# Batch 0 of a fused attention and feed-forward kernel: batch 1's q and k projected ahead of the row scores, four steps of transposed scores beside the row maxima

## The reference, cut to what matters

```python
q, k, v = (embedded @ W.T + b).reshape(b, s, H, HD).transpose(0, 2, 1, 3)   # for each of Wq, Wk, Wv
...
p = jax.nn.softmax(einsum('bhqd,bhkd->bhqk', q, k) / sqrt(s), axis=-1)
p = p * jnp.triu(jnp.ones((s, s)), k=0)
z = einsum('bhqk,bhkd->bhqd', p, v)
x = layernorm(x + layernorm(x + z) * gamma + beta)
h = silu(tlin(x, w1_w, w1_s)) * tlin(x, w2_w, w2_s)
h = gelu(tlin(h, h1_w, h1_s)); h = gelu(tlin(h, h2_w, h2_s))
out = layernorm(x + tlin(h, w3_w, w3_s))
```

## Time and profile before

| what | value |
|---|---|
| median of three runs | 1188.02 us (1187.51 to 1189.85) |
| span of the profiled execution | 1187.2 us (the only time listed for it) |
| TensorE, VectorE, ScalarE, GpSimd busy | 97%, 66%, 42%, 34% |
| share of the chain that ended last | TensorE 93%, VectorE 4%, DMA 1%, ScalarE 1% |
| batch 0: first row scores | 22.5 us |
| batch 0: last row maxima end | 62.4 us |
| batch 0: first values begin, last end | 67.3, 104.7 us |
| batch 0: feed-forward begins | 117.3 us |

### The profile page before, as it was taken

The page is one execution under the profiler, slowest core; times in us unless marked ns, Lnnn a source line. Parts: engine busy times, 40 slices in busy tenths (PEclk is TensorE's granted clock), DMA queues, the critical chain, the costliest instruction groups (busy, mean ns, idle before and its releaser), DMA issues.

```text
span 1187.2 us, 18377 instructions
## 1 busy us (share of the span) xinstructions
PE 1149.0 (97%) x7311; PEld 809.2 (68%) x7311; DVE 784.1 (66%) x1276; ACT 492.9 (42%) x660; POOL 401.8 (34%) x373
## 2 busy tenths in 40 slices
PE   6499999999999999999999999999999999999997
PEld 3255778667785777757777577866778577775886
DVE  5986773778737776487755777377873777648513
ACT  4475312762138511574117631276213751156311
POOL 1343423144222632235222352315332262212432
PEclk8589999999999999999999999999999999999999
DMA  8971332422224422323244133242222432232000
GB/s 303 338 208 59 112 82 56 108 97 82 73 55 109 142 69 53 87 67 141 72 91 108 55 120 78 55 108 105 74 73 56 109 142 71 48 69 68 1 1 18
DMA packets 44954, 111.71 MB, mean 94 GB/s; under 512 B 8000, under 2 KB 19648, under 8 KB 44864
## 3 DMA queue, kind: packets, MB, share of 16 engines
q1 hardware_dynamic: 40016, 98.01, 29.2%
q10 hardware_dynamic: 4848, 12.47, 3.1%
HBM read 88.95 MB, written 21.50 MB: 93 GB/s over the span
## 4 chain that ended last, share of the span: by engine, by line
PE 93%; DVE 4%; DMA 1%; ACT 1%; issue 1%; POOL 0%; SPq 0%; POOLq 0%; ACTq 0%
PE PS L1244 54%; PE PS L1156 11%; PE PS L1180 7%; PE PS L1120 6%; PE PS L1063 5%; PE PS L1187 3%; PE PS L1193 2%; DVE neg_max L784 2%; PE PS L1080 2%; DMA stacks<-qk_rows 1%; ACT probsT L678 1%; PE PS L1209 1%; PE PS L1344 1%; DMA qk_rows<-qk_lo 0%; PE PS L1288 0%
## 5 line engine op out<-in xcount | busy, mean ns | idle before, releaser
L777 DVE TENSOR_REDUCE neg_max<-PS 128x3 f32<-128x1536 f32 (+1 forms) x168 | 256.9, 1574 | 61.9 <-PE PS L1120 61.9
L540 POOL TENSOR_TENSOR hidA_lo<-hidA_full,hidA_hi 128x512 fp32r<-128x512 f32 x128 | 174.1, 1360 | 225.6 <-DVE hidA_hi L1024 180.5
L678 ACT ACTIVATE probsT<-PS 128x1024 f32<-128x1024 f32 x192 | 184.6, 1023 | 53.4 <-PE PS L1156 49.3
L1244 PE MATMUL PS<-hidA_hi,g 128*128 128x512 f32 x512 | 205.5, 401 | 0.4 <-POOL hidA_lo L540 0.4
L1244 PE MATMUL PS<-hidC_hi,g 128*128 128x512 f32 x512 | 203.0, 397 | 0.0
L1244 PE MATMUL PS<-hidA_lo,g 128*128 128x512 f32 x512 | 199.9, 391 | 0.0
L1244 PE MATMUL PS<-hidC_lo,g 128*128 128x512 f32 x512 | 199.7, 390 | 0.0
L540 POOL TENSOR_TENSOR hidC_lo<-hidC_full,hidC_hi 128x512 fp32r<-128x512 f32 x64 | 82.2, 1285 | 202.0 <-DVE hidC_hi L1024 202.0
L1156 PE MATMUL PS<-stacks 66*128 66x512 f32 x512 | 147.3, 418 | 1.6 <-DVE neg_max L784 1.1
L699 ACT ACTIVATE hidC_full<-PS,scales 128x512 f32<-128x512 f32 x64 | 44.2, 690 | 243.1 <-PE PS L1244 243.1
L699 ACT ACTIVATE hidA_full<-PS,scales 128x512 f32<-128x512 f32 x64 | 44.1, 689 | 218.6 <-PE PS L1244 218.6
(11 more groups left out here) (131 smaller groups left out, 1650.4 us busy)
## 6 DMA issues: line engine op xcount, KB each, us to landing
stacks<-qk_rows SPq DMA_DIRECT2D x124, 256.0 KB
stacks<-qk_rows SPq DMA_DIRECT2D x246, 128.0 KB
qk_rows<-qk_hi SPq DMA_DIRECT2D x16, 512.0 KB, 2.7
qk_rows<-qk_lo SPq DMA_DIRECT2D x16, 512.0 KB, 2.9
xT_sb<-xT_dram SPq DMA_DIRECT2D x8, 512.0 KB, 4.0
g_raw<-h1T_dram ACTq DMA_DIRECT2D x4, 1024.0 KB, 12.1
g_raw<-h2T_dram ACTq DMA_DIRECT2D x4, 1024.0 KB, 16.7
x_tok<-x_dram SPq DMA_DIRECT2D x8, 512.0 KB, 5.0
```

What stands on the lines that cost most here:

```text
L540: nc.gpsimd.tensor_tensor(lo[:, m, :], full[:, m, :], hi[:, m, :], ALU.subtract).then_inc(lo_done, 1)
L678: nc.scalar.activation(probs(s)[:, 2 * pair:2 * pair + 2, :], PS[:, bank:bank + 2, :], ACT.Exp, scale=SCALE).then_inc(exp_done, 1)
L777: ins = nc.vector.tensor_reduce(NEGM[:, half, at:at + hi - lo], PS[:, bank:bank + hi - lo, :], AX.X, ALU.max, negate=True)
L1244: ins = nc.tensor.matmul(out, d if swapped else w, w if swapped else d, start=(k == 0 and part == 0), stop=(k == kts - 1 and part == 1))
```

## The change

Only the part around batch 0 changes.

- q and k of batch 1 are projected right behind v of batch 0, from an own tile `xT_next` loaded at the start; ScalarE adds the bias (`bias_next`), GpSimd takes the low part (`split_next`), SyncE stores them behind the stack loads, to a second half of the DRAM tensor.
- For head groups 0 and 1 only the transposed stacks are loaded (into `stacks`); the row scores are taken from them too, head by head, both sides from rows 0 to 63.
- Row scores and maxima are in 32 units of one query tile (two sides, two banks, one VectorE instruction of the same size as before), in buffers at banks 4 and 6, with bank 2 as a third in units 6 to 17. The first half of the maxima is turned behind unit 17, not behind the ninth unit of 16.
- The transposed scores of pairs 0 to 7 are issued behind units 22 to 29, one each. ScalarE's exponentials of them stand between weight tests 9 and 14, one test behind every second. They need the maxima's rows, which four small DMAs a group now copy from SBUF to SBUF (`load_first_max`), behind the stores of batch 1's q and k on SyncE's queue.
- GpSimd rounds the six late pieces, between steps 7 and 11; VectorE tests four of them ahead of its norms and two behind those of head group 0.
- Behind the values, batch 0 has v of batch 1 between and behind the last two steps, then the turn of x2, six `keep_warm` products, and the first two tiles of the first layer in two parts, as batch 7 has three.
- One weight load is issued later at the start (`load_pair(1)`), and four in place of three in advance.

The diff, cut to its core:

```diff
-AHEAD = 3
+AHEAD = 4
...
-FIRST_UNITS = H
 PAIRS = NQUAD * 2 * QT
+FIRST_UNITS = PAIRS
+FIRST_STEPS = 4
+SCORES_FROM = 22
+TESTS_BEFORE = 10
...
-        START_BANKS = (0, 4)
+        ROW_BANKS = [(2, 4, 6)[u % 3] if 6 <= u < 18 else (4, 6)[u % 2] for u in range(FIRST_UNITS)]
+        TURN_BANKS = (0, 5)
...
+    XT1 = place("xT_next", [P, DT, S], F32, C)
+    SQ1 = place("first_squares", [P, 2, S], F32, C + 4 * KB)
+    QK1f = place("next_qk_full", [P, 2 * DT, S], F32, C + 8 * KB)
+    QK1lo, QK1lo_f = both("next_qk_lo", [P, 2 * DT, S], C + 24 * KB)
...
+            sp.dma_start(XT1[:], xT[D:2 * D, :].rearrange("(t p) s -> p t s", p=P)).then_inc(next_xT_in, 16)
...
+            def load_first_max(group):
+
+                half, place = divmod(group, 2)
+                sp.wait_ge(max_split, half + 1)
+                for r in range(2):
+                    for side in range(2):
+                        at = MAXES // 2 * side + MAXES // 4 * place
+                        sp.dma_start(ST_f[SPLIT + r:SPLIT + r + 1, group % 2, 0, 2 * side:2 * side + 2, :].rearrange(
+                            "r pair (t p) -> r (pair t) p", p=P),
+                                     MROW_f[at:at + MAXES // 4, half, r, :]).then_inc(first_max_in[group % 2], 16)
...
+            load_q_turned(sp, 0, 0)
+            sp.wait_ge(k_stored, 2 * 16)
+            load_k_turned(sp, 0, 0, 0)
+            sp.wait_ge(stack_in[0], LOADS_S)
+            load_q_turned(sp, 0, 1)
             for r1 in range(2):
-                load_q_rows(sp, first_stack, 0, r1, stack_in[0])
-            sp.wait_ge(k_stored, 2 * 16)
-            load_k_rows(sp, first_stack, 0, 0, stack_in[0])
-            sp.wait_ge(stack_in[0], LOADS_S)
-            load_stacks(0, 1, False)
+                load_k_turned(sp, 0, 1, r1)
             for g in range(2, NQUAD):
-                load_rows(lambda rows: RST_f[rows, g - 2, :, :], g, first_rows_in[g - 2])
-            load_stacks(0, 0, True)
-            store_max(0, 0)
-            load_max(0, 0)
-            load_stacks(0, 1, True)
-            load_max(0, 1)
+                load_rows(0, lambda rows: RST_f[rows, g - 2, :, :], g, first_rows_in[g - 2])
+            store_rows(1)
+            load_first_max(0)
+            load_first_max(1)
...
-                    store_max(b, 1)
                     load_stacks(b, 2, True)
-                    load_max(b, 2)
                     load_xT()
                     load_stacks(b, 3, True)
-                    load_max(b, 3)
-                    store_rows(b + 1)
...
+            def bias_next(n):
+
+                act.wait_ge(qk_proj, 2 * DT + n + 1)
+                nc.scalar.activation(QK1f[:, n, :], PS[:, n, :], ACT.Identity, bias=BQK[:, n:n + 1])
+                nc.scalar.activation(QKhi[:, n, :], PS[:, n, :], ACT.Identity,
+                                     bias=BQK[:, n:n + 1]).then_inc(qk_biased, 1)
...
+            load_pair(0)
             act.wait_ge(bqk_in, 16)
             for n in range(2 * DT):
                 act.wait_ge(qk_proj, n + 1)
                 nc.scalar.activation(QKhi[:, n, :], PS[:, bank_qk(n), :], ACT.Identity,
                                      bias=BQK[:, n:n + 1]).then_inc(qk_biased, 1)
+            load_pair(1)
             for n in range(2 * DT):
-                square_qk(0, n)
+                square_first(0, n)
+            sum_lost(0)
+            sum_lost(1)
             act.wait_ge(k_stored, 2 * 16)
-            load_k_rows(act, first_stack, 0, 1, stack_in[0])
-            for n in range(BEFORE):
+            load_k_turned(act, 0, 0, 1)
+            act.wait_ge(q_stored, 2 * 16)
+            act.wait_ge(squared, 2 * DT)
+            bias_next(0)
+            bias_next(1)
+            act.wait_ge(stack_in[0], LOADS_S)
+            for pair in range(EARLY, EARLY + AHEAD):
+                load_pair(pair)
+            act.dma_start(SC[:], scales.rearrange("p (n t) -> p n t", n=4)).then_inc(consts_in, 16)
+            for t, src in ((GAM, gamma), (BET, beta), (S3, s3)):
+                act.dma_start(t[:], src.rearrange("(a d) -> a d", a=1).to_broadcast([P, D])).then_inc(consts_in, 16)
+            bias_next(2)
+            bias_next(3)
+            for n in range(2 * DT):
+                square_first(1, n)
+
+            def test_piece(n):
+
                 sum_lost(n)
-                if n == 2 * EARLY - 1:
-                    act.wait_ge(stack_in[0], LOADS_S)
-                    for pair in range(EARLY, EARLY + AHEAD):
-                        load_pair(pair)
-                    act.dma_start(SC[:], scales.rearrange("p (n t) -> p n t", n=4)).then_inc(consts_in, 16)
-                    for t, src in ((GAM, gamma), (BET, beta), (S3, s3)):
-                        act.dma_start(t[:], src.rearrange("(a d) -> a d", a=1).to_broadcast([P, D])).then_inc(consts_in, 16)
-                elif n % 2 and n >= 2 * EARLY and n // 2 + AHEAD < len(PIECES) // 2:
+                if n % 2 and n >= 2 * EARLY and n // 2 + AHEAD < len(PIECES) // 2:
                     load_pair(n // 2 + AHEAD)
+
+            for n in range(EARLY, TESTS_BEFORE):
+                test_piece(n)
+            for pair in range(2 * FIRST_STEPS):
+                if pair == 2:
+                    act.wait_ge(qk_split, 4 * DT)
+                if pair == 6:
+                    act.wait_ge(q_stored, 4 * 16)
+                    act.wait_ge(k_stored, 4 * 16)
+                exps(0, pair // 2, pair % 2)
+                if pair % 2:
+                    test_piece(TESTS_BEFORE + pair // 2)
+            for n in range(TESTS_BEFORE + FIRST_STEPS, BEFORE):
+                test_piece(n)
...
-                i, half = divmod(unit, 2)
-                for side in sides:
-                    at = side * PAIRS // 2 + i % 4 * QT + 2 * half
-                    nc.vector.tensor_reduce(NEGM[:, i // 4, at:at + 2],
-                                            PS[:, bank + 2 * side:bank + 2 * side + 2, :], AX.X, ALU.max,
-                                            negate=True).then_inc(maxed, 1)
+                half, at = divmod(unit, PAIRS // 2)
+                bank = ROW_BANKS[unit]
+                nc.vector.tensor_reduce(NEGM[:, half, at:at + PAIRS // 2 + 1:PAIRS // 2],
+                                        PS[:, bank:bank + 2, :], AX.X, ALU.max, negate=True).then_inc(maxed, 2)
...
-                    for n in range(0, LATE, 2):
+                    for n in range(LATE - 2):
                         test_late(n)
-                        test_late(n + 1)
-                        round_late(n)
-                        round_late(n + 1)
                     dve.wait_ge(lost_summed, BEFORE)
-                    dve.wait_ge(late_summed, LATE)
-                    nc.vector.tensor_reduce(LOST1[:], LOST[:, 0:len(PIECES)], AX.X, ALU.add).then_inc(lost_row_summed, 1)
...
+            def project_next(n):
+
+                if n < DT:
+                    pe.wait_ge(qk_biased, n + 1)
+                    pe.wait_ge(qk_split, n + 1)
                 else:
-                    pairs = range(2 * unit, 2 * unit + 2)
+                    pe.wait_ge(v_taken, 1)
+                w, c = (WQ, WK)[n // DT], n % DT
+                for k in range(DT):
+                    ins = nc.tensor.matmul(PS[:, n, :], w[:, k, c * P:(c + 1) * P], XT1[:, k, :],
+                                           start=(k == 0), stop=(k == DT - 1))
+                ins.then_inc(qk_proj, 1)
...
+                        if b == 0 and group < 2:
+                            ins = nc.tensor.matmul(PS[:, base + side, :],
+                                                   ST[0:SPLIT, group, 0, 2 * side + pair, qt * P:(qt + 1) * P],
+                                                   ST[0:SPLIT, group, 1, 2 * side + pair, :], start=True, stop=True)
+                            continue
...
+            pe.wait_ge(next_xT_in, 16)
+            for n in range(2 * DT):
+                project_next(n)
             pe.wait_ge(consts_set, 5)
             for unit in range(FIRST_UNITS):
-                if unit == FIRST_UNITS // 2:
+                row_scores(0, unit)
+                if unit == FIRST_UNITS // 2 + 1:
                     pe.wait_ge(ident_in, 16)
-                row_scores(0, unit, behind_turn=unit == FIRST_UNITS // 2 + 1, banks=START_BANKS)
-                if unit == FIRST_UNITS // 2:
-                    turn_max(0, 0, FIRST_UNITS, START_BANKS[1])
-            scores_T(0, 0)
-            turn_max(0, 1, 2 * FIRST_UNITS, 6)
-            for s in range(1, LAG):
-                scores_T(0, s)
+                    pe.wait_ge(qk_biased, 4 * DT)
+                    turn_max(0, 0, FIRST_UNITS, TURN_BANKS[0])
+                if 0 <= unit - SCORES_FROM < 2 * FIRST_STEPS:
+                    scores_pair(0, unit - SCORES_FROM)
+            turn_max(0, 1, 2 * FIRST_UNITS, TURN_BANKS[1])
+
+            def first_attention():
+
+                done = 0
+                for p in range(2 * FIRST_STEPS, 2 * STEPS):
```

(26 more changed lines are left out.)

237 lines of the change are left out of this document (142 added, 95 removed).

## The result

The changed kernel takes 1200.78 us (median of four runs, 1200.41 to 1201.23) against 1188.84 for the kernel before (four runs, 1187.51 to 1189.85): a ratio of 1.0106, 95% interval 1.0094 to 1.0118. It is slower by 12 us; 1184.4 was predicted. The spans of the profiled executions are 1187.2 and 1199.5.

A forecast was written before the change was run, and what follows sets the result against it. TensorE was taken to bound nearly all the span once batch 0's feed-forward starts. Attention ending 0.8 us later and 4.4 gained in the tail start it 3.6 earlier: 1188.0 - 3.6 = 1184.4 us, range 1180.3 to 1189.5.

The forecast's parts named there:

- Step 1: Up to scoring the first pair: the maxima's rows land at 53.0 us, range 50.3 to 58.
- The eight products of batch 1's q and k: Ahead of unit 0: some 4 us at full clock, hidden in TensorE's 6.69 us wait for the first stack.
- The wait on the rows: Ahead of pair 0: maxima's rows queue behind 1.14 MB more on SyncE's queue; 53.0 us against 50.3 without wait.
- Step 2: From pair 0 to first values: ScalarE's exponentials and tests take 3.0 us per two units; values start 18.2 us later, at 71.2.
- part (b) of the prediction: Eight of batch 0's 32 score pairs, moved between the row scores, take 4.2 us off TensorE's path.
- Step 3: Batch 0's attention: 34.3 us from first to last values, ending at 105.5, 0.8 later; neither ScalarE nor VectorE binds.
- Step 4: The tail behind the last values, to two feed-forward tiles done, net: 8.2 us against 12.6, 4.4 gained.
- a slow clock: In the tail: a clock of 0.50 could add up to 1.7 us for half the products; 0.6 was taken.
- Slower: the queue: Rival at SyncE's queue: the maxima's rows land after 58.8; landing at 60 gives 1191.4 us; chance 0.12.
- The clock is back when the values begin: Rival at the first values: 2.4 GHz again, worth 1.4 us, total 1183.0; chance 0.15 beside whichever other case holds.
- The rule against the shared form of the scores: Row scores of units 0 to 15: 0.6 to 1.0 us each, showing only in units 0 to 5, at most 0.05 each.

The follow-up runs named there:

- e8: e5 with head groups 0 and 1 loaded in the layout of the row scores again and their transposed stacks loaded behind; 1203.02 us.
- e12: e8 with group 0's maxima rows ahead of the stores, T1 and group 1's rows, and exponentials waiting for stores only where they overwrite; 1194.53 us.
- e1: The changed kernel with the second weight load (w2) issued at the start again; 1201.17 us.
- e9: The changed kernel with e1's edit and batch 1's q and k computed from batch 0's x, without the extra 0.5 MB load; 1199.21 us.
- e5: e3 with e1's edit and three weight loads issued in advance in place of four; 1197.53 us.
- e2: The changed kernel with the maxima's rows ahead of the stores of batch 1's q and k on SyncE's queue; 1199.52 us.
- e4: The changed kernel with ten products on all 128 rows, read by nobody, ahead of pair 0 inside TensorE's wait; 1197.59 us.
- e3: The changed kernel with no score pairs beside the maxima; the eight pairs and their exponentials stand behind the last row scores; 1197.54 us.
- e6: The changed kernel with all six late weight tests ahead of VectorE's norms; 1201.58 us.
- e7: e5 with e6's edit and unread 128-row products behind each unit from 16 on and between the first pairs; 1201.53 us, ratio 1.011 to the kernel before.

## Why the prediction was wrong

Its four steps against the trace, the feed-forward's start being their sum:

| step | predicted | measured | off by |
|---|---|---|---|
| 1: maxima's rows landed | 53.0 | 61.34 | +8.3 |
| 2: from there to the values | 18.2 | 21.5 | +3.3 |
| 3: to the end of the last values | 34.3 | 37.5 | +3.2 |
| 4: to two tiles done, less 3.6 | 8.2 | 8.8 | +0.6 |

15.4 us together turn 3.6 earlier into 11.8 later.

**Step 1 failed, the largest part, and mostly at a point that it did not work out.** It took everything up to the split at 45.05 as unchanged and counted bytes only from 24 us on. The eight products of batch 1's q and k, put at some 4 us, took 7.0 at the full clock (16.13 to 23.16), which is more than the 6.7 us wait that was to hide them; they were hidden only because the first stack came later still (in e8 0.6 us of idle time is left behind them, in e12 none). The first stack was later: by 1.8 us for the second weight load, now issued just ahead of the stores and stacks instead of at the start (e1); by 1.3 for the load of batch 1's x (e9 against e1); by 1.25 for the turned form of the stack (e8 against e5). That is 4.4, the whole of the 4.35. Each was read from one pair of kernels, but the kernels fall together by what their fronts do: 26.7 to 27.7 in all five that have both loads late and the turned form, 24.8 to 25.2 in the three with w2's load at its old place, 23.6 in the three that have the row form as well. No run had the row form without the load of x. The stack of group 1 lost more to its form: 3.6 us from e5 to e8 at 34 to 38 us. Group 1's 6.6 us are 1.8 from the loads (changed kernel to e5), 3.6 from the form and 1.2 that is left in e8, and the 6.7 at the split is these together. The turned form has the same bytes in as many DMAs; but while it comes in, the full DMA engines move 299 GB/s in all, and 414 while the other does (e5, e8). Why was not taken apart. The wait on the rows was named with the right cause of the earlier trace rows, 9.6 us from split to landing where I had 7.9. Only 1.85 of it is the stores that I had charged for (e2).

**Step 2: the wrong engine.** I had ScalarE bound at 3.0 us for two units, 1.5 each; it was TensorE at 1.87, at half the clock. The numbers for it stood in the earlier trace rows: 2.04 for two pairs and 0.6 for a unit's row scores give 1.6 and more, above 1.5. I didn't add them for the interleaved stretch. e4 shows the size: at the full clock a unit takes 1.10 and ScalarE is waited for, as the step said. e3 shows the consequence: four steps beside the maxima cost 4.4 us at the end of the attention, where part (b) of the prediction had put a gain.

**Step 3: the bound again.** That VectorE does not bind either was wrong. GpSimd's first mask begins 17.9 us later, VectorE's first scaled matrix 14.1 later (92.56), and from there it is VectorE's own chain, 28.3 us to the last head group. In the kernel before the same stretch, 78.47 to 104.77, was 26.3. Two tests in its middle are 1.3 of that (e6). The pairs taken off TensorE did shorten the stretch, by 2.9 us for five against e3 (40.4 to 37.5), but they had cost 7.3 ahead of it. Not separated from VectorE's chain is the clock, which stayed at half for the first 5 us of the values (to 88) and before for 3 (to 70): no run takes the two apart.

**Step 4 was nearly right**, 3.8 us gained for 4.4: batch 1's k and q no longer stand in the tail. The branch took 2.42 us of issue for 1.91, and VectorE took up the last head group 0.4 us behind the last values, before 0.07. It is in part luck: 0.6 had been set aside for a slow clock, which was 1.00 here from 110 to 140 us, so the rest came out 1.2 larger than put.

**The rivals.** "Slower: the queue" named the place and the side, and put the price at 1191.4: it counted one wait and not the later front. "The clock is back when the values begin" rested on TensorE being busy there; it was, 15.46 of 16 us from 61 to 77, and the clock stayed at 0.50. The rule against the shared form of the scores was priced at 0.05 us in six units; its products in fact fill TensorE (7.99 of 8 us from 40 to 48), but eight units took 8.34 us, 1.04 each, under VectorE's 1.14, and the cost lay in loading that form.

Open: what brings the clock up (ten products on all rows did in e4, more of them did not in e7) and what sets it in the tail from one kernel to the next (from 120 to 130 us 1.00 after, 0.66 in e6, both with similar products); and whether batch 1's q and k could be had ahead without their DMA traffic; e12 is the nearest, and its attention still waits on stacks.
